# Split sums for ten mean products, weight units fetched into idle tiles, two buffers for split attention values

## What is computed

```python
h = xf @ W_proj + b_proj                       # (2048, 1024)
y = layernorm(h) * g + b
w = softmax(y @ W_wgen + b_wgen)               # 8 heads x 5 taps
conv = sum_k w[k] * shift(y, k)                # causal, within a sequence of 64
h = h + relu(conv @ W_ff + b_ff)
q, k, v = split(layernorm(h) @ w_qkv.T + b_qkv)   # 8 heads of 64, 32 sequences of 64
h = h + causal_attention(q, k, v) @ w_o.T + b_o
t = layernorm(h)[:, perm]                      # 16 heads of 64
h = h + (gelu(t @ up) @ down)[:, unperm]
```

## Time and profile before

| | |
|---|---|
| median of 3 runs | 966.39 us (962.8 to 966.87) |
| the profiled execution | 968.3 us |
| its span, first to last instruction | 965.9 us |
| mean granted TensorE clock | 0.991 |
| TensorE busy | 943.1 us (98%), 6108 matmul records |
| VectorE busy | 540.3 us (56%) |
| ScalarE busy | 438.3 us (45%) |
| GpSimd busy | 387.6 us (40%) |
| products of L339 to L341 on the chain that ended last | 58% |

### The profile page before, as it was taken

The page is one execution under the profiler, slowest core; times in us unless marked ns, Lnnn a source line. Parts: engine busy times, 40 slices in busy tenths (PEclk is TensorE's granted clock), DMA queues, the critical chain, the costliest instruction groups (busy, mean ns, idle before and its releaser), DMA issues.

```text
span 965.9 us, 15776 instructions
## 1 busy us (share of the span) xinstructions
PE 943.1 (98%) x6108; PEld 707.5 (73%) x6108; DVE 540.3 (56%) x887; ACT 438.3 (45%) x774; POOL 387.6 (40%) x312
## 2 busy tenths in 40 slices
PE   9999999998999999999999999999999999999996
PEld 8778787776877788788778878878887766623342
DVE  5254544878658312356475266257064479788773
ACT  6244444482754543436253243244132232287874
POOL 1224242523752221823560550451023157487742
PEclk9999999999999999999999999999999999999999
DMA  7750605128354254149002002100124985634521
GB/s 259 279 177 1 224 1 211 33 92 257 115 181 125 88 150 161 45 160 336 5 12 99 22 12 61 60 13 23 42 79 143 259 302 201 260 116 137 170 105 76
DMA packets 54383, 122.99 MB, mean 127 GB/s; under 512 B 16283, under 2 KB 17307, under 8 KB 49830
## 3 DMA queue, kind: packets, MB, share of 16 engines
q1 hardware_dynamic: 49190, 105.22, 32.7%
q0 software_dynamic: 5120, 16.78, 5.1%
HBM read 79.37 MB, written 42.60 MB: 126 GB/s over the span
## 4 chain that ended last, share of the span: by engine, by line
PE 79%; DVE 6%; DMA 6%; issue 3%; POOL 2%; ACT 2%; SPq 1%; POOLq 0%; DVEq 0%; ACTq 0%
PE bank L339 20%; PE bank L341 19%; PE bank L340 19%; PE bank L1978 6%; PE bank L1962 3%; PE bank L1706 2%; DMA h<-h_s 2%; PE bank L1687 1%; DVE h L1489 1%; DVE sq L420 1%; DMA stage<-w_proj 1%; PE bank L1965 1%; DMA stage<-w_ff 1%; PE bank L1863 1%; PE bank L1836 1%
## 5 line engine op out<-in xcount | busy, mean ns | idle before, releaser
L375 POOL TENSOR_TENSOR vacc<-vacc,sq 128x512 f32<-128x512 f32 x72 | 97.4, 1353 | 44.9 <-ACT sq L425 33.3
L339 PE MATMUL bank<-cv_h,wf_h 128*128 128x512 f32 x256 | 105.2, 411 | 3.2 <-POOL wf_l L333 3.2
L339 PE MATMUL bank<-xa_h,wp_h 128*128 128x512 f32 x256 | 102.5, 400 | 0.1
L341 PE MATMUL bank<-cv_h,wf_l 128*128 128x512 f32 x256 | 100.5, 393 | 0.0
L340 PE MATMUL bank<-cv_l,wf_h 128*128 128x512 f32 x256 | 100.5, 392 | 0.0
L341 PE MATMUL bank<-xa_h,wp_l 128*128 128x512 f32 x256 | 100.4, 392 | 0.0
L340 PE MATMUL bank<-xa_l,wp_h 128*128 128x512 f32 x256 | 100.3, 392 | 0.0
L768 POOL TENSOR_TENSOR fo<-fo,res 128x512 f32<-128x512 f32 x32 | 44.1, 1392 | 100.2 <-ACT fo L910 75.2
L1170 ACT ACTIVATE gt<-bank 128x512 f32<-128x512 f32 x128 | 66.0, 603 | 33.6 <-PE bank L1962 20.1
L1978 PE MATMUL bank<-gt,dn_f 128*64 128x512 f32 x256 | 61.8, 604 | 0.0
L425 ACT ACTIVATE sq<-sq 128x512 f32<-128x512 f32 x56 | 34.6, 637 | 59.7 <-DVE sq L420 59.7
(11 more groups left out here) (194 smaller groups left out, 2240.2 us busy)
## 6 DMA issues: line engine op xcount, KB each, us to landing
xs<-x_t SPq DMA_DIRECT2D x32, 256.0 KB, 6.1
h_s<-ho SPq DMA_DIRECT2D x8, 1024.0 KB, 4.3
res<-h_s SPq DMA_DIRECT2D x32, 256.0 KB, 3.6
h_s<-fo SPq DMA_DIRECT2D x32, 256.0 KB, 2.5
dc<-h_s SPq DMA_DIRECT2D x4, 2048.0 KB, 9.0
h<-h_s SPq DMA_DIRECT2D x8, 1024.0 KB, 10.7
h_s<-h SPq DMA_DIRECT2D x8, 1024.0 KB, 6.1
band_s<-zero SPq DMA_DIRECT2D x4, 1096.0 KB, 8.5
```

The lines of the kernel that those rows point to most:

```text
L339: pe.matmul(o, wh, xh, start=start, stop=False)
L341: return pe.matmul(o, wl, xh, start=False, stop=stop)
L375: g.tensor_tensor(vacc[:, :], t[:, 0, :] if k == 1 else vacc[:, :], t[:, at, :], ALU.add).then_inc(ln_vac, 1)
```

## The change

- Means and variances: ten products with `mean_w` become two fp32r products each, on a sum that is split into `sum_h` (ScalarE) and a low part written over the sum (VectorE). These are the four means of `a_step` and the first convolution, and mean and variance of chunks 1 to 3 of the attention's layer norm. `mean_r` is `mean_w` as fp32r. In the first attention step the mean moves from ahead of the scores into the second `c_qk`, behind block 0, and the variance from block 3 to block 5 of the third.
- Units `U_FF + 4` to `U_FF + 7` are fetched into the four tiles `fo`, in the last `a_step`, ahead of `band_skew(2)` on SP's queue; `b_load(1)` goes ahead of the remaining unit loads, and the slots of `stage` are free for the next four.
- `vs_h` and `vs_l` become pairs, used in turn. Split values of chunk c+1 are made while chunk c is computed, behind the seventh centering and square, instead of behind the evacuation of group 1.
- The row variance goes to bank 7 and behind the mean of group 0; its root on ScalarE ahead of the squares.
- `RAW` is 8 instead of 9 (a semaphore less), `zero_ok` goes into `masks_ok`, some waits are added for the tiles that are used anew.

```diff
@@ -90,6 +91,9 @@
         rstd = place("rstd", [P, N], F32, LNT + 8 * KIB)
+        sum_h = place("sum_h", [P, N], F32R, LNT + 8 * KIB)
+        acc_l = place("acc_l", [P, N], F32R, LNT)
+        vacc_l = place("vacc_l", [P, N], F32R, LNT + 6 * KIB)
         mean3 = place("mean3", [P, N], F32, LNT + 8 * KIB)
...
@@ -145,8 +149,8 @@
         wo_r = place("wo_r", [P, PAIRS, D], F32, R2 + 16 * KIB)
-        vs_h = place("vs_h", [P, PAIRS, N], F32R, R1 + 16 * KIB)
-        vs_l = place("vs_l", [P, PAIRS, N], F32R, R1 + 24 * KIB)
+        vs_h = [place(f"vs_h{i}", [P, PAIRS, N], F32R, R1 + (16 - 8 * i) * KIB) for i in range(2)]
+        vs_l = [place(f"vs_l{i}", [P, PAIRS, N], F32R, at) for i, at in enumerate((R1 + 24 * KIB, E + 24 * KIB))]
         vs = place("vs", [P, PAIRS, N], F32, E + 16 * KIB)
...
@@ -304,8 +309,16 @@
+        def unit_early(e, i):
+
+            e.wait_ge(w_ld[i], slot_count(U_FF + i))
+            e.dma_start(fo[i][:, :], units[U_FF + 4 + i][0]).then_inc(w_ld[i], 16)
+
         def unit_load(e, u):
-            if u >= 4:
+            if U_FF + 8 <= u < U_FF + 12:
+                e.wait_ge(w_lo_v, lo_before[0][u - 7])
+                e.wait_ge(w_ld[u % 4], slot_count(u - 4))
+            elif u >= 4:
...
@@ -319,6 +332,8 @@
             raw = units[u][4] if u >= U_V else stage[:, u % 4, :]
+            if U_FF + 4 <= u < U_FF + 8:
+                raw = fo[u - U_FF - 4][:, :]
             return raw, units[u][1], units[u][2]
...
@@ -347,7 +362,35 @@
+        def split_index(L, var):
+
+            return (L if L < CH else 2 * L - 6) + (1 if var else 0)
+
+        def sum_high(act, L, var):
+            if var:
+                since(act, ln_vac, L, 7, 7)
+            else:
+                since(act, ln_sum, L, 7, 7)
+            act.activation(sum_h[:, :], (vacc if var else acc)[:, :], ACT.Copy).then_inc(sum_hi, 1)
+
+        def sum_low(v, L, var):
+            full, low = (vacc, vacc_l) if var else (acc, acc_l)
+            v.wait_ge(sum_hi, split_index(L, var) + 1)
+            v.tensor_tensor(low[:, :], full[:, :], sum_h[:, :].bitcast(F32), ALU.subtract).then_inc(sum_lo, 1)
+
+        def split_mean_pe(pe, L, var, b):
+            pe.wait_ge(sum_lo, split_index(L, var) + 1)
+            if L == 0:
+                pe.wait_ge(masks_ok, 17)
+            pe.matmul(bank[b][:, :], mean_r[:, :], sum_h[:, :], start=True, stop=False)
+            pe.matmul(bank[b][:, :], mean_r[:, :], (vacc_l if var else acc_l)[:, :],
+                      start=False, stop=True).then_inc(ln_var if var else ln_mean, 1)
+
         def ln_mean_pe(pe, L):
+            if L > CH:
+                since(pe, ln_std, L - 1, 1, 1)
+                split_mean_pe(pe, L, False, LN_BANK)
+                return
             since(pe, ln_sum, L, 7, 7)
...
@@ -380,8 +423,11 @@
         def ln_var_pe(pe, L):
+            since(pe, ln_d, L, 8, 8)
+            if L > CH:
+                split_mean_pe(pe, L, True, LN_BANK)
+                return
             since(pe, ln_vac, L, 7, 7)
-            since(pe, ln_d, L, 8, 8)
             pe.matmul(bank[LN_BANK][:, :], mean_w[:, :], vacc[:, :], start=True, stop=True).then_inc(ln_var, 1)
...
@@ -412,6 +458,8 @@
                 since(e, st_copied, S, 1, 1)
+            if 2 * CH < L < 3 * CH - 2 and k < 2:
+                since(e, ln_vac, L - 1, 7, 7 if k else 6)
             if L == 3 * CH - 1:
...
@@ -562,17 +610,21 @@
                     stat_store(c - 1, 1)
+                    if c == CH - 1:
+                        sp.wait_ge(ln_vac, 7 * c)
+                        sp.wait_ge(ln_d, 8 * c)
+                        sp.wait_ge(mean_st, 16 * c)
+                        for i in range(4):
+                            unit_early(sp, i)
                     band_skew(c - 1)
...
-            for u in range(U_FF + 4, U_FF + 6):
-                unit_load(sp, u)
             b_load(1)
-            for u in range(U_FF + 6, U_FF + 10):
+            for u in range(U_FF + 8, U_FF + 12):
                 unit_load(sp, u)
             band_load(1)
-            for u in range(U_FF + 10, U_V):
+            for u in range(U_FF + 12, U_V):
                 unit_load(sp, u)
...
@@ -907,6 +961,8 @@
                 since(act, fo_st[m % 4], c, 32, 16 * (m // 4))
+                if c == 0 and m < 4:
+                    act.wait_ge(w_lo_g, lo_before[1][U_FF + 8])
                 act.activation(fo[m % 4][:, :], bank[m][:, :], ACT.Relu,
...
@@ -924,6 +980,7 @@
                 y_high(n, 1, ho)
+                sum_high(act, n, False)
                 y_high(n, 2, ho)
...
@@ -963,6 +1020,8 @@
                     conv_high(0, h - 1)
+                if h == SPLIT_AFTER:
+                    sum_high(act, CH - 1, False)
             act.wait_ge(ln_mean, CH)
...
@@ -1087,21 +1146,27 @@
                     since(act, vs_ld, c, 16, 16)
-                    released(act, c - 1, k, PAIRS, vs_used, o_mm)
+                    if c > 1:
+                        act.wait_ge(o_mm, 8 * (c - 1))
                     src = vs0 if c == 0 else vs
-                    act.activation(vs_h[:, k, :], src[:, k, :], ACT.Copy).then_inc(vs_hi, 1)
+                    act.activation(vs_h[c % 2][:, k, :], src[:, k, :], ACT.Copy).then_inc(vs_hi, 1)
...
                 later = not (isinstance(c, int) and c == 0)
+                if ahead and not later:
+                    sum_high(act, c + 1 + CH, False)
                 c_softmax_exp(c, 0)
...
                     c_vals(c - 1, PAIRS - 1)
-                    c_values(c, range(TILES))
+                    c_values(c, (0, 1))
+                    if ahead:
+                        sum_high(act, c + 1 + CH, False)
+                    c_values(c, (2, 3))
                 if ahead and later:
...
@@ -1114,6 +1179,7 @@
                 if ahead:
+                    sum_high(act, c + 1 + CH, True)
                     c_std(c + 1)
...
@@ -1148,12 +1214,14 @@
                     stat_copy_act(act, L, CH + c - 2)
+                    if c > 1:
+                        row_std_act(act, L - 1, VAR_BANK)
                     for k in range(KB if c < CH - 1 else 0):
                         stat_square_act(act, L, k)
-                if c + 1 < CH:
+                        if k == VALUES_AFTER:
+                            vs_high(c + 1, range(PAIRS))
+                if c == 0:
                     vs_high(c + 1, range(PAIRS))
-                if 0 < c < CH - 1:
-                    row_std_act(act, L, VAR_BANK)
...
@@ -1285,8 +1354,10 @@
             def a_stats(n):
-                for k in range(3):
+                for k in range(2):
                     y_low(n, k, ho)
+                sum_low(v, n, False)
+                y_low(n, 2, ho)
                 for k in range(KB):
...
@@ -1338,6 +1409,7 @@
                     ff_low(0)
+                    sum_low(v, CH - 1, False)
             for i in range(1, 4):
...
@@ -1446,19 +1518,24 @@
                     src = vs0 if c == 0 else vs
-                    v.tensor_tensor(vs_l[:, k, :], src[:, k, :], vs_h[:, k, :].bitcast(F32),
+                    v.tensor_tensor(vs_l[c % 2][:, k, :], src[:, k, :], vs_h[c % 2][:, k, :].bitcast(F32),
                                     ALU.subtract).then_inc(vs_lo, 1)
...
                 later = not (isinstance(c, int) and c == 0)
+                if ahead and not later:
+                    sum_low(v, c + 1 + CH, False)
                 c_softmax_in(c, 0)
                 c_softmax_out(c, 0)
+                if ahead and later:
+                    sum_low(v, c + 1 + CH, False)
                 if ahead:
...
                 if ahead:
+                    sum_low(v, c + 1 + CH, True)
                     since(v, ln_std, c + 1 + CH, 1, 1)
...
@@ -1544,6 +1621,8 @@
                             o_sum(c, [k - 3])
+                        if k >= VALUES_AFTER:
+                            o_low(c + 1, range(2 * (k - VALUES_AFTER), 2 * (k - VALUES_AFTER) + 2))
                     if c >= 2:
...
@@ -1554,12 +1633,10 @@
                         d_scale(0, k)
-                if c + 1 < CH:
-                    o_low(c + 1, range(PAIRS - 1))
+                if c == 0:
+                    o_low(c + 1, range(PAIRS))
                 o_evac(c, A_GROUPS[2])
                 o_sum(c, range(SUM_SPLIT if c in (0, CH - 1) else 3, KB))
-                if c + 1 < CH:
-                    o_low(c + 1, [PAIRS - 1])
...
@@ -1642,7 +1719,7 @@
                             pe.wait_ge(a_ev, 8 * c)
-                            stat_mean_pe(pe, c - 1)
+                            split_mean_pe(pe, c - 1, False, LN_BANK)
                         if (g, k) == (1, 4 if c < CH - 1 else 5):
...
@@ -1869,18 +1946,16 @@
                 later = not (isinstance(c, int) and c == 0)
-                if not later:
-                    ln_mean_pe(pe, c + 1 + CH)
                 c_scores(c, 0)
...
                     ln_mean_pe(pe, c + 1 + CH)
-                c_qk(c, 1)
```

(15 more changed lines are left out.)

25 lines of the change are left out of this document (14 added, 11 removed).

## The result

The changed kernel takes 967.0 us (median of 20 runs, 964.7 to 971.8), the kernel before 965.2 in the same comparison (20 runs, 962.7 to 967.8). The ratio is 1.0027, 95% interval 1.0015 to 1.0038. The forecast was 960.7, the range 954.5 to 964.8: wrong, by 6.3 us, and outside the range. The forecast took 5.7 us off 966.4, the median of three runs of the kernel before; over 20 runs that kernel takes 965.2. So a gain of 5.7 us was forecast, and 1.8 us were lost. The profiled execution spans 969.8 us (before 965.9), at a mean granted clock of 0.992; TensorE is busy for 939.1 us of it (before 943.1), so it works less and waits more.

The account below looks back on a forecast made before the run. TensorE was taken as the bound, busy nearly all the span. Terms 1.2 + 4.3 + 0.3 + 1.6 - 1.7 = 5.7 us off the 966.4 median gave 960.7 us, range 954.5 to 964.8.

Parts of the forecast that it names:

- Three means of the projection, +1.2: `a_step`: three float32 means become split products, each gaining 0.41 us, 1.2 in all; bounds -2 to +1.2.
- means and variances of chunks 2 and 3, +1.6: Attention stage: two means and two variances as split products gain 4 x 0.41 = 1.6 us; bounds -1 to +1.6.
- Rival 3: Attention chunks 1 to 3: TensorE waits at the split variances and the clock falls, 969.9 us; chance 6%.
- Early units and first convolution, +4.3: First convolution and feed-forward: early weights gain 4.95 us, the convolution's split mean costs 0.65; bounds 2.6 to 5.4.
- the whole 4.95 goes, nothing takes its place: First feed-forward: the `wf_l` wait of 3.2 us and its 1.7 us of clock vanish without a new wait.
- even odds nearly: First convolution: chance that the clock falls behind the longer `ar` wait, up to 1.7 us more, taken as none.
- Attention chunk 1, +0.3: Attention chunk 1: split mean and variance, moved later, gain 0.3 us in all; bounds -1 to +1.7.
- 0.6 idle: Attention chunk 1: TensorE at 471.65 waits 0.6 us for the split mean, ready near 472.2.
- Output stage, -1.7: Output projection: old `vs_l` waits go, new waits for sums of 3.4 and 2.3 us come; 1.7 us lost, bounds +7.5 to -3.
- the two waits of 1.9 us and their clock, 3.7 us each: Output projection: two waits of 1.9 us, each with 1.7 us of clock, are removed by the change.
- no earlier than TensorE comes: End of output stage: chunk 3's residual load moves by 1.9 us, letting the feed-forward start at about 838, when TensorE arrives.
- Rival 2: Relocated waits dearer: convolution wait pulls the clock (1.7 us), split sums late at places (0.5 each); about 964, chance 18%.

Follow-up runs that it names:

- before_again: The kernel before, unchanged, run and profiled once more; ratio 1.0011 to the kernel before, profiled span 962.2 us.
- raw8_only: The kernel before with `RAW` 8 for 9 and nothing else; ratio 1.0005 to the kernel before.
- out_only: The kernel before with the output stage's part of the change alone (second pair of split-value buffers, row variance in bank 7); ratio 1.0043.
- buf_only: The kernel before with the second pair of split-value buffers alone, row variance left in bank 3 and its old place; ratio 1.0051.
- a_means_only: The kernel before with `RAW` 8 and the three split means of the first stage alone; ratio 1.0009.
- combo: The changed kernel with the old output stage, `RAW` 9, relus 3 to 5 ahead of `y_base`, and chunk 1's split variance behind block 4; ratio 0.9957.
- combo_fo: combo with the four early weight loads moved behind the first stage's last stores, ahead of `b_load(1)`; ratio 0.9949 to the kernel before.
- combo_c1: combo with mean and variance of attention chunk 1 as one float32 product each in their old places; ratio 0.9942 to the kernel before.
- after_again: The changed kernel, unchanged, run and profiled once more; ratio 1.006 to the kernel before, profiled span 967.4 us.
- undone_relu: The changed kernel with the old output stage and relus 3 to 5 of chunk 0 ahead of `y_base` on ScalarE; ratio 0.9971.
- undone_raw9: The changed kernel with the output stage as before and `RAW` 9; ratio 0.9951 to the kernel before.
- early_only: The kernel before with `RAW` 8 and the early weight units alone, including the `b_load(1)` that moves with them; ratio 0.9981.
- undone_b1_late: The changed kernel with the old output stage and `b_load(1)` put back behind the loads of units 8 to 11; ratio 0.9974.

## Why the prediction was wrong, step by step

Means of the table stand for each term, since one execution is off by a draw of the clock. Where old code runs: the profile of before, before_again, raw8_only, out_only, buf_only.

- *Three means of the projection, +1.2*: right. 1.26 less 0.11 is 1.15 in the changed kernel, 1.15 in a_means_only, 1.13 to 1.16 in the others. So were *means and variances of chunks 2 and 3, +1.6*: 1.51 to 1.63 in twelve of the thirteen executions that have them (1.36 in the other), and nobody waits at `vacc_l`, where 0.1 us was to spare. Rival 3, slower, had the sign right by a mechanism that is refuted.
- *Early units and first convolution, +4.3*: the step "the whole 4.95 goes, nothing takes its place" failed. The wait did go. Measured are 0.62 to 1.56 us in the five executions with this code (1.16 in the mean), and the old code is 0.36 slower on average than its first profile: 1.5 us gained, 2.8 fewer than forecast. Three things took the place, none of them in the working. The gap in the convolution costs 1.2 us (combo against combo_fo). The wait for the relus 3 to 5 behind `y_base` costs 1.4 us where the clock stays up (1.56 gained in the changed kernel, 2.96 with the relus first). The clock, which I had at "even odds nearly" and took as nothing, fell in three of the five executions (0.84, 1.33 and 0.62 gained) and not in two (1.56, 1.43): 0.6 us there, since a TensorE that is late anyway waits less for the next consumer; with the relus first it costs its whole 1.6 us (combo 1.19, combo_c1 2.76). I had asked whether the four issues delay SP's queue, not whether the transfers meet others; and I had followed the `wf_l` wait's own chain to its end, but not the next consumer, although ScalarE's order for it stands in the code.
- *Attention chunk 1, +0.3*: the step "0.6 idle" and the "about 0.2" left over behind the reciprocal were mis-sized. Six executions with the split at block 5 and `RAW` 8 lost 1.0 to 3.35 us, 2.1 in the mean, where the old code with `RAW` 9 had gained 0.4: minus 2.5. The late variance makes TensorE wait 0.78 and about 0.7 us for `qk` in every one of them, and where nothing else waits this alone loses 1.0 us (after_again 1.00, undone_relu 0.99, undone_raw9 1.04). The rest is the wait for the split sum, which differs between executions: 1.96, 1.54, 1.19, 0.34 us and twice none, where the working has 0.6. The mechanism was named, the size was off by 2.8 us.
- *Output stage, -1.7*: the waits were forecast at 3.4 and 2.3 us and measured at 3.10 and 2.21, with half rate behind both, and 0.48 for `vs_l`. The term measured -4.6: thirteen executions with the old stage are 1.5 us shorter there on average than the first profile, the five with the new one 3.1 longer (-4.2 to -5.1 by time). Two steps failed. First, what the waits were weighed against, "the two waits of 1.9 us and their clock, 3.7 us each": half rate followed the old waits in 16 of 26 cases, not in all, and all ten new ones. At the end of the projection the old stage stands 1.6 us ahead of its first profile, the new one 2.2 behind it, so 3.8 apart, where 1.7 was forecast. Second, "no earlier than TensorE comes", by which the feed-forward starts without loss: the loss there is 0.8 us on average, in the changed kernel's profile 1.9. VectorE stood idle for 7.75 us until the residual came at 833.06, TensorE waited 0.86 us for its evictions at 840.08 and 1.16 for `gt` at 851.3.
- The sum by these: 1.15 + 1.5 - 2.5 + 1.55 - 4.6 = -2.9 us, a loss; measured was a loss of 1.8 (967.0 less 965.2), and 5 in the second, smaller set of runs. Rival 2 named two of the parts (the clock behind the first convolution, late split sums) at less than half their size. The result lies within 0.5%, to which I had given 40%, but on the other side of no change than the working had it.

Three smaller slips changed little. The earlier trace rows do not show an activation "right behind" the table load; in that trace the next one starts 6.42 us behind it. The changed kernel has the case, and the 1.28 us held, with nothing more:

```profile
793.69 1.28 ACT L508 ACT_TABLE_LOAD   x1
794.99 0.68 ACT L508 ACTIVATE srow<-bank,eps 1x512 f32<-1x512 f32 x1
```

That "four issues of 0.7 delay nothing" was off by 1.2 us: the fourth issue came 3.4 us behind the third, and the `wk` stores began at 198.88 for 197.69. And seven tenths of 50% and 22% is 57%, not 56.

What stays open: why the first 43 us differ by up to 3.8 us between kernels that are nearly the same there (7 products at half rate in before and before_again, 13 in the changed kernel, none in twelve of the twenty); what decides whether the clock falls behind a wait of 1.5 to 2 us; the gap at 456.56; and, since the means above rest on five to thirteen executions of different kernels, how the 1.8 us divide exactly.

## What to carry to other kernels

A wait in one profile has a price in time and a second one in clock, and the second is drawn anew in each execution: credit a removed wait of 1.9 us with a part of the clock's 1.6 us, not all of it (16 of 26 here), and charge a new one of 2.1 to 3.1 us with all of it (10 of 10). Where TensorE is busy 97% of the span, a removed wait is worth only what the next consumer's chain allows: follow the queue of each engine beyond the place, to the wait that is late next. Data fetched early share the DMA engines with the instructions: look at the instruction queue before a load is moved into a busy stretch. Splitting a small float32 product pays 0.4 us where its input is ready early, and loses several times that where the input arrives with the consumer or where other engines' work stands behind it.

## What the runs showed of the hardware

- Half rate follows waits of 1.5 to 1.95 us in some executions of a kernel and not in others: 5 of 9 behind the `ar` wait (1.75 to 1.78 us), 5 of 13 and 11 of 13 behind the `vs_l` waits (1.89 to 1.93). Behind the 1.1 us wait for `ar` it never came, in nine executions; behind the `acc` waits of 2.1 to 3.1 us and the `wf_l` waits of 2.5 to 3.3 it came in all sixteen. It did not come behind single waits of 2.02 (early_only, `acc`) and 2.59 us (buf_only, `h`).
- A queue with many small stores ahead holds large ones: the ten stores of `wk` took 6.22 to 6.32 us to issue in nineteen traces and 14.65 in one. From 196 to 200 us the DMA engines of undone_b1_late show a share of 1.09 at 23 GB/s.
- TensorE can stand still for 0.9 to 1.8 us in the middle of like products with nothing to wait for. Eleven such gaps end 1.2 to 1.5 us behind the end of a 16 KB block of an instruction queue, which had set out 1.0 to 4 us late beside full DMA engines; one more (456.56, combo) has no such block.
- A VectorE operation on two SBUF tiles that starts beside a GpSimd one ends 0.55 us behind it, in 70 of the 74 slowed ones of the changed kernel's trace (0.56 in the others): 1.77 to 1.79 us for 0.74 in `y_prep`.
